# Layer 3 of an edge network turned round: edges on partitions instead of features

## The reference, cut to what matters

```
msg = concat([x_i, x_j - x_i])                  # 200000 x 64
h = relu(msg @ W1 + b1)                         # 64 -> 64
h = relu(h @ W2 + b2)                           # 64 -> 128
h = relu(h @ W3 + b3)                           # 128 -> 64
m = h @ W4 + b4                                 # 64 -> 32
s = segment_sum(m, i_idx); cnt = segment_sum(ones, i_idx)
x = layernorm(x + s / maximum(cnt, 1)[:, None])
```

## Time and profile before

| | |
|---|---|
| median of 3 runs | 1571.46 us (1568.09 to 1571.53) |
| profiled execution, first to last instruction | 2441.1 us (the profile gives no other time of it) |
| mean granted TensorE clock, profiled | 0.764 of 2.4 GHz |
| PE busy, profiled | 1767.5 us |
| DVE busy, profiled | 947.9 us |
| ACT busy, profiled | 602.6 us |
| POOL busy, profiled | 1125.9 us |

### The profile page before, as it was taken

How to read it: one execution, slowest core, us unless ns; L and a number is a source line. 1 busy time by engine, 2 the same in 40 slices (tenths; PEclk the granted TensorE clock), 3 DMA queues, 4 the chain that set the end, 5 groups by cost and what they waited for, 6 DMA issues and landing times.

```text
span 2441.1 us, 39243 instructions
## 1 busy us (share of the span) xinstructions
PE 1767.5 (72%) x13131; PEld 1040.0 (43%) x13131; DVE 947.9 (39%) x3086; ACT 602.6 (25%) x945; POOL 1125.9 (46%) x1165
## 2 busy tenths in 40 slices
PE   3133777777768777878787778786867778777797
PEld 2112444444444444444444444444444444444454
DVE  3663343333333343333333333443333333333356
ACT  2233122222212222212222222222221222122234
POOL 5275444453544454354545454544444454444411
PEclk7555787877878787777778877777877877787888
DMA  5334643343434443353434353544344344444332
GB/s 128 98 93 88 200 112 112 106 140 94 136 101 116 126 121 109 103 147 91 135 105 136 104 152 92 152 109 114 104 123 115 111 114 109 133 118 118 109 106 59
DMA packets 189929, 283.06 MB, mean 116 GB/s; under 512 B 84614, under 2 KB 90169, under 8 KB 189156
## 3 DMA queue, kind: packets, MB, share of 16 engines
q1 hardware_dynamic: 152341, 241.67, 33.7%
q0 software_dynamic: 36704, 37.00, 7.3%
q10 hardware_dynamic: 682, 1.85, 0.3%
HBM read 266.51 MB, written 13.73 MB: 115 GB/s over the span
## 4 chain that ended last, share of the span: by engine, by line
PE 63%; issue 23%; another core or an unknown queue 6%; DVE 3%; ACT 2%; DMA 1%; SPq 1%; DVEq 0%; POOL 0%; ACTq 0%; POOLq 0%
PE ps L964 22%; PE ps L996 12%; PE ps L988 10%; PE ps L1019 5%; PE ps L1004 4%; PE ps L919 3%; PE ps L901 3%; PE ps L1016 2%; PE ps L978 2%; ACT work L716 1%; ACT work L731 1%; DMA sums<-in_src 1%; DVE region L1410 0%; DVE region L1292 0%
## 5 line engine op out<-in xcount | busy, mean ns | idle before, releaser
L585 POOL DMA_INDIRECT xj<-z_rows,src_t x1107 | 1074.5, 971 | 1190.9 <-PE ps L919 787.7
L964 PE MATMUL ps<-region,x_p 128*96 128x150 bf16 (+53 forms) x5876 | 569.6, 243 | 416.6 <-issue 407.2
L964 PEld LDWEIGHTS ps<-region,x_p 128*96 128x96 bf16 x5876 | 440.6, 142 | 572.9 <-issue 566.7
L731 ACT ACTIVATE work<-ps,b3s 128x512 f32<-128x512 f32 x196 | 134.7, 687 | 1335.5 <-PE ps L996 1037.1
L996 PE MATMUL ps<-work,w3s 128*64 128x512 f32 x784 | 356.6, 840 | 21.2 <-issue 21.1
L1377 DVE TENSOR_SCALAR region<-region,cst 128x1565 bf16<-128x1565 int16 (+6 forms) x416 | 245.7, 634 | 268.0 <-remote 256.3
L988 PE MATMUL ps<-work,w2s 64*128 64x512 f32 x784 | 298.1, 827 | 6.8 <-ACT work L716 5.6
L724 ACT ACTIVATE work<-ps,b2s 128x512 f32<-128x512 f32 x392 | 250.7, 684 | 161.0 <-PE ps L988 82.7
L1392 DVE COPY work<-ps 128x512 f32<-128x512 f32 x194 | 133.4, 687 | 336.4 <-PE ps L1004 217.0
L1386 DVE CAST work<-ps 96x512 bf16<-96x512 f32 x52 | 35.7, 686 | 513.9 <-PE ps L964 506.8
L1410 DVE TENSOR_SCALAR region<-iota_g,dst_rel 128x42 f32<-128x42 f32 x1120 | 185.7, 250 | 0.0
(11 more groups left out here) (156 smaller groups left out, 826.3 us busy)
## 6 DMA issues: line engine op xcount, KB each, us to landing
dstb<-dst_rows SPq DMA_DIRECT2D x196, 252.0 KB
region<-src_rows SPq DMA_DIRECT2D x104, 391.2 KB
region<-src_rows SPq DMA_DIRECT2D x52, 407.2 KB
region<-src_rows SPq DMA_DIRECT2D x52, 403.2 KB
region<-src_rows SPq DMA_DIRECT2D x52, 376.2 KB
region<-src_rows SPq DMA_DIRECT2D x52, 375.8 KB
region<-src_rows SPq DMA_DIRECT2D x52, 374.0 KB
region<-src_rows SPq DMA_DIRECT2D x52, 366.2 KB
```

The lines of the kernel that those rows point to most:

```text
L585: pool.indirect_dma_start(out=xj[:, u, j % UT, j // UT, 0:w], out_offset=None, in_=rows, in_offset=bass.IndirectOffsetOnAxis(ap=cols[:, j: ...
L964: chosen = nc.tensor.matmul(ps[0:XP, XBANK[h], lo - h * UE:hi - h * UE], xb[:, a, :], hot[:, q % QN, at + lo:at + hi], start=not begun[h], ...
```

## The change

Each tile of 128 edges of layer 2's output becomes the stationary operand, and W3 (64 columns) moves. Layer 3 then comes out with edges on partitions, 8 matmuls a step into one of two banks, and needs no transpose. relu(y + b3) is written as max(y, -b3) + b3: VectorE takes the maximum against a tile `floor3` of -b3 while it copies, and b3 x W4 is added to b4 once, by one matmul and five small VectorE instructions (`last_weights`). relu3 and ScalarE's copies are gone. The summing of a window moves from three steps behind to two, the pipeline is one step shorter, and VectorE does the maximum and the adding at the head of its step. `stay_busy` has other counts at the end.

```diff
-        p_x, p_h1, p_h3 = ps[:, 0, :], ps[:, 1, :], ps[:, 4, :]
+        p_x, p_h1 = ps[:, 0, :], ps[:, 1, :]
-        p_ht = ps[:, 5, :]
+        p_h3 = ps[:, 4:6, :].rearrange("p v (t h f) -> p v t h f", t=UT, h=2)
+        p_b4 = ps[H3:H3 + 1, 7, 256:256 + O]
...
+            sp.dma_start(floor3[:, :], b3.unsqueeze(0).to_broadcast([P, H3])).then_inc(s_w, 16)
...
@@ scalar: step @@
-                if 2 <= s < AHEAD:
-                    copy_layer3(s - 2)
-                if s >= 1:
-                    relu3(s - 1)
@@ tensor @@
             def layer3(s):
-                if s >= 1:
-                    pe.wait_ge(s_r3, s)
+                if s >= 2:
+                    layer3_copied(pe, s - 2)
                 for h in range(2):
                     pe.wait_ge(s_r2[h], s + 1)
-                    nc.tensor.matmul(p_h3[h * H3:(h + 1) * H3, :], w3s[:, :], h2[:, s % 2, h, :],
-                                     start=True, stop=True).then_inc(s_l3, 1)
-
-            def turn_layer3(s):
-                pe.wait_ge(s_r3, s + 1)
-                if s >= 1:
-                    layer3_copied(pe, s - 1)
-                for t in range(UT):
-                    turned = nc.tensor.transpose(p_ht[:, t * T:(t + 1) * T], h3[:, s % 2, t * T:(t + 1) * T], ident)
-                turned.then_inc(s_ht, 1)
+                    for t in range(UT):
+                        made = nc.tensor.matmul(p_h3[:, s % 2, t, h, :], h2[:, s % 2, h, t * T:(t + 1) * T], w3s[:, :],
+                                                start=True, stop=True)
+                made.then_inc(s_l3, 1)
...
-                stay_busy({S_N + 1: 3}.get(s, 0))
-                if 2 <= s <= S_N + 1:
-                    turn_layer3(s - 2)
-                stay_busy({S_N: 4, S_N + 1: 2, S_N + 2: 8}.get(s, 0))
-                if s >= 3:
-                    sum_window(s - 3)
+                stay_busy({S_N: 4, S_N + 1: 6}.get(s, 0))
+                if s >= 2:
+                    sum_window(s - 2)
...
+            pe.wait_ge(s_w, 16 * 16)
+            nc.tensor.matmul(p_b4, b3s[0:H3, :], w4s[0:H3, :], start=True, stop=True).then_inc(s_b4, 1)
...
-                for s in range(AHEAD, S_N + 3):
+                for s in range(AHEAD, S_N + 2):
@@ vector @@
+                nc.vector.tensor_scalar(floor3[:, :], floor3[:, :], -1.0, None, ALU.mult).then_inc(s_ready, 1)
+
+            def last_weights():
+                dve.wait_ge(s_b4, 1)
+                link(nc.vector.tensor_tensor(w4s[H3:H3 + 1, :], w4s[H3:H3 + 1, :], p_b4, ALU.add))
                 link(nc.vector.tensor_reduce(w4mean[:, :], w4s[:, 0:O], AX.X, ALU.add))
                 link(nc.vector.tensor_scalar(w4mean[:, :], w4mean[:, :], -1.0 / O, None, ALU.mult))
...
             def copy_layer3(s):
-                dve.wait_ge(s_ht, s + 1)
+                dve.wait_ge(s_l3, s + 1)
                 if s >= 2:
                     dve.wait_ge(s_agg, s - 1)
-                nc.vector.tensor_copy(h3t[:, s % 2, :, :, 0:H3], p_ht.rearrange("p (t h f) -> p t h f", t=UT, h=2))\
+                nc.vector.tensor_tensor(h3t[:, s % 2, :, :, 0:H3], p_h3[:, s % 2, :, :, :],
+                                        floor3[:, :].unsqueeze(1).unsqueeze(1).to_broadcast([P, UT, 2, H3]), ALU.max)\
                     .then_inc(s_h3c, 1)
...
             def step(s):
+                if 2 <= s <= S_N + 1:
+                    copy_layer3(s - 2)
+                if s >= 3:
+                    add_sums(s - 3)
                 if s < S_N and is_sorted(s):
                     copy_x(s)
-                if AHEAD <= s <= S_N + 1:
-                    copy_layer3(s - 2)
                 if s + 1 < S_N:
                     build_pick(s + 1)
-                if 2 <= s <= S_N + 1:
-                    build_onehot(s - 2)
-                if s >= 3:
-                    add_sums(s - 3)
+                if 1 <= s <= S_N:
+                    build_onehot(s - 1)
```

More of the change, by code:

```diff
@@ L163, in build @@
         b3s = sb("b3s", [P, 1], F32)
+        floor3 = sb("floor3", [P, H3], F32)
         ring_at = 4 * PT * WIN + 4 * PE2
@@ L220, in build @@
         x16 = part(work[:, :].bitcast(BF16), 12 * UE, (2, UE))
-        h3 = part(work, 8 * UE, (2, UE))
         h3t = part(work, 10 * UE, (2, PT * (H3 + 1))).rearrange("p v (t h f) -> p v t h f", t=UT, h=2)
@@ L296, in build @@
         s_l2 = [sem(f"layer2_unit{n}") for n in range(2)]
-        s_l3, s_ht, s_agg = sem("layer3"), sem("layer3_turned"), sem("window_summed")
-        s_h3a = sem("layer3_copied_by_scalar")
+        s_l3, s_agg = sem("layer3"), sem("window_summed")
         s_pick, s_oh, s_h3c, s_acc = sem("pick_built"), sem("onehot_built"), sem("layer3_copied"), sem("sums_added")
@@ L301, in build @@
         s_moved, s_centre = sem("windows_moved"), sem("centring_chain")
-        s_r1, s_r3 = sem("relu1"), sem("relu3")
+        s_r1 = sem("relu1")
         s_r2 = [sem(f"relu2_unit{n}") for n in range(2)]
@@ L307, in build @@
         s_open = sem("pass_open")
+        s_b4 = sem("bias_through_w4")
         s_begun = sem("gathers_begun")
@@ L364, in layer3_copied @@
         def layer3_copied(eng, s):
[L366 to L369, removed]
+            eng.wait_ge(s_h3c, s + 1)
         def even_rows(n):
@@ L683, in _ @@
                 split_more(g)
-            act.wait_ge(s_w, 15 * 16)
+            act.wait_ge(s_w, 16 * 16)
             act.wait_ge(s_set, 2)
@@ L722, in relu2 @@
                     if s >= 2:
-                        act.wait_ge(s_l3, 2 * (s - 1))
+                        act.wait_ge(s_l3, s - 1)
                     nc.scalar.activation(h2[:, v, h, :], p_h2[:, h, :], ACT.Relu, bias=b2s[:, 0:1]).then_inc(s_r2[h], 1)
[L726 to L738, removed]
             def step(s):
@@ L1179, in weights @@
             def weights():
-                dve.wait_ge(s_w, 15 * 16)
+                dve.wait_ge(s_w, 16 * 16)
                 w = w1par[0:XP, :]
@@ L1185, in weights @@
                 nc.vector.tensor_tensor(w1p[0:XP, 2, :], w, w1p[0:XP, 1, :], ALU.subtract)
+                nc.vector.tensor_scalar(floor3[:, :], floor3[:, :], -1.0, None, ALU.mult).then_inc(s_ready, 1)
+            def last_weights():
+                dve.wait_ge(s_b4, 1)
+                link(nc.vector.tensor_tensor(w4s[H3:H3 + 1, :], w4s[H3:H3 + 1, :], p_b4, ALU.add))
                 link(nc.vector.tensor_reduce(w4mean[:, :], w4s[:, 0:O], AX.X, ALU.add))
                 link(nc.vector.tensor_scalar(w4mean[:, :], w4mean[:, :], -1.0 / O, None, ALU.mult))
-                nc.vector.tensor_scalar(w4s[:, 0:O], w4s[:, 0:O], w4mean[:, 0:1], None, ALU.add).then_inc(s_ready, 1)
+                link(nc.vector.tensor_scalar(w4s[:, 0:O], w4s[:, 0:O], w4mean[:, 0:1], None, ALU.add))
             def subtract_part0(h):
@@ L1388, in copy_layer3 @@
             def copy_layer3(s):
-                dve.wait_ge(s_ht, s + 1)
+                dve.wait_ge(s_l3, s + 1)
                 if s >= 2:
                     dve.wait_ge(s_agg, s - 1)
-                nc.vector.tensor_copy(h3t[:, s % 2, :, :, 0:H3], p_ht.rearrange("p (t h f) -> p t h f", t=UT, h=2))\
+                if s == 0:
+                    dve.wait_ge(s_ready, 1)
+                nc.vector.tensor_tensor(h3t[:, s % 2, :, :, 0:H3], p_h3[:, s % 2, :, :, :],
+                                        floor3[:, :].unsqueeze(1).unsqueeze(1).to_broadcast([P, UT, 2, H3]), ALU.max)\
                     .then_inc(s_h3c, 1)
@@ L1464, in _ @@
             count_passes()
+            last_weights()
             dve.wait_ge(s_end, 1)
```

## The result

The kernel after took 1633.8 us (1631.2 to 1639.3, 4 runs) where the kernel before took 1569.8 (1568.1 to 1571.5): 1.042 times as long, 95% interval 1.039 to 1.045, some 64 us more. The forecast was 15 us more. This time the profile did not disturb the run: its span is 1631.2 us.

The account below looks back on a forecast made before the run. The prediction took gather issue on GpSimd as the bound before, passing narrowly to TensorE: 1492 + 78 (longer steps) + 16 (waits) + 2.5 (start) - 3.4 (end) = 1585 us, own range 1573 to 1605, wider range 1560 to 1660.

Parts of the forecast that it names:

- What bounds the kernel before: Whole kernel before: issue of gathers on GpSimd bounds it, their sum 1566 to 1589 us, TensorE about 80 us short.
- TensorE alone: TensorE's work without waiting for gathers: 1492 us in the kernel before, 1585 us in the kernel after.
- The pair of 128-column load and 64-column stream: New layer 3 on TensorE: 16 pairs at 0.112 us, 1.94 us up to layer 2 where 1.16 stood.
- case E: Rival for the new layer 3: weight load and stream take turns, 0.16 us a pair, 1732 us; chance 3%.
- D: Rival: the 128-column pair goes at the summing pair's 0.057 us and TensorE is the bound, 1480 us; chance 8%.
- The waits of the summing for the adding: TensorE's summing waits for VectorE's maximum and adding: 0.12 us in steps after a gathered window, 16 us together.
- The start and the end: Before the loop 2.5 us more (0 to 6); after the last step 3.4 us less, for one stage fewer.
- The gathers alone: 1571 + 2.5 - 3.4 = 1570.: Time of the kernel after if only the gathers bound it: 1570 us, with start and end changes.
- VectorE does not get longer: VectorE's maximum in layer 3 taken at 0.69 us, the same as the copy it replaces.
- case B: Rival: the gathers stay the bound after the change, 1570 us, no change; chance 26%.
- C: Rival: TensorE was the bound already, for a reason outside the stretch read, 1664 us; chance 13%.
- if the time rises by over 60 us (then TensorE was the bound before): Sign that the forecast is wrong: a rise over 60 us would mean TensorE bound the kernel before.

Follow-up runs that it names:

- kernel before once more: The kernel before, unchanged, run again for a trace that the profiler does not disturb: 1571.0 us, trace span 1569.1 us.
- the sorted stretch with few gathers: Kernels before and after, each cut to 2 gathers a step instead of 8 from the 11th gathered step on: 1411.6 and 1532.8 us; stretch from first to last sorted step.

## Why the prediction was wrong, point by point

**What bounds the kernel before.** Right in kind: the gathers, shown by 1.5 us of waiting on one side and 113 on the other. Its sum was right by two errors that cancelled. I took 205.4 us as the start of the loop's gathers from the disturbed execution; in the undisturbed one the first gather of the loop, the 97th, starts at 155.4. And I took 1.25 to 1.27 us a gather from the disturbed trace; it is 1.30. TensorE alone was off by its own start: it enters step 5's selection at 162.7 us (kernel before once more), not at 247.9. It needs 1412 us, not 1492, so it had 160 us to spare, not 80.

**The pair of 128-column load and 64-column stream.** Right: 16 of them and the gap took 1.91 us where 1.94 was forecast, and a whole gathered step 5.03 where 4.99 was. Load and stream run side by side; case E (2.7 us by its 0.16 a pair) falls, and D too.

**The waits of the summing for the adding.** Right: 13.3 us in the sorted stretch with few gathers, forecast 15. The whole stretch grew by 100 us, forecast 90.

**The start and the end.** Mis-sized: 15 us later with TensorE alone instead of 2.5, and 7 us more at the end. They cost next to nothing in the result, since the gathers begin almost as early as before (the 97th at 155.4 and 156.1) and from the last gather to the end are 45.7 us where 44.5 were; of the 3.4 us that the shorter pipeline was to save nothing shows.

**"The gathers alone: 1571 + 2.5 - 3.4 = 1570."** This is the step that failed. It held the time of a gather fixed while the change moved VectorE's instructions, and I gave no price to the new order: "VectorE does not get longer" was true and beside the point. It measured 1.307 us a gather before and 1.362 after, 61 us, and this is what the gathers lost beside runs of source one-hots (65.6, less 4.5 won elsewhere). The old kernel with that order alone loses the same 4.2%, and one pause ahead of the runs takes it all back. So the bound did not pass to TensorE. My case B had the right engine and, with 1570, the wrong time; C was near the time (1664) for a reason that the trace of before refutes. That the measured 1634 lies inside my wider range of 1560 to 1660 is luck: its part above 1605 was there for C. My sign "if the time rises by over 60 us (then TensorE was the bound before)" misled too: it rose by 64, and GpSimd was the bound before and after.

**What stays open.** A gather that begins at one distance from a run waits and one that begins at another doesn't: in the kernel after none of the 25 that began about 0.5 us into a run was long. What decides this inside a gather no run shows, nor why the adding right ahead of the run mostly lets a gather in and window one-hots don't, nor why 5 of 12 are long behind the adding in the kernel before. That a pause acts on the gathers by how it changes the run's start is read from the table above, and no run varied the pause's length.

## What to carry to other kernels

When GpSimd issues the transfers that bound a kernel, VectorE's order is part of its price: look for gathers longer than the median and for what VectorE runs beside them, before asking how long VectorE is busy. Here a run of 16-bit SBUF-to-SBUF instructions that followed other VectorE work without a pause made gathers wait for its end; one wait of VectorE for its own last instruction, put ahead of the run, ended that, at the price of 9.5 us on an engine that has time. And a profile that is 55% longer than the runs can be right in its dense stretches and wrong in its starts by 50 and 85 us: take a second one before adding to its starts.

## What the runs showed of the hardware

A DMA_INDIRECT of 128 rows on GpSimd took 0.944 us undisturbed and started every 1.25. Beside a run of three VectorE tensor_scalar instructions (128x1465 to 1629, int16 to bf16, 1.68 us for three) it took up to 2.83: the long ones did not get their turn between two of the three, though each is an instruction of its own. This happened to 41 of the 54 gathers that started within 0.15 us of a run's start when the run followed other tensor_scalar instructions directly, and to none of 68 when 0.04 us of pause lay between.

An fp32 matmul with 128 stationary and 64 moving columns went at about 0.11 us a pass with its load, (1.98 - 0.28) / 15. At the pace of the summing rows with 84 moving columns (0.073) a stream of 64 would need 0.056, so the load seems to set it; that is an inference from these rows.
